# A recurrent layer with an FFN gate on eight cores: the scan's carry is copied by VectorE instead of ScalarE

## The reference

```python
xn = layernorm(x)                                   # over the 1024 features
# linear recurrence with complex states, one per p of 1024
Lambda = exp(-exp(nu_log) + 1j * exp(theta_log))
Bu = einsum('ph,blh->blp', (B_re + 1j*B_im) * exp(gamma_log)[:, None], xn)
xs = scan over l of  s[l] = Lambda * s[l-1] + Bu[l]
s  = einsum('hp,blp->blh', C_re + 1j*C_im, xs).real + D * xn
# gate
g  = silu(relu(xn @ W1 + b1) @ W2 + b2)             # 1024 -> 4096 -> 1024
out = x + s * g
```

## Time and profile before

| | us |
|---|---|
| two timed runs | 4930.87 and 5070.12, median 5000.49 |
| the profiled execution | 4701.79 |
| its span, slowest core (core 4) | 4700.7 |
| spans of the eight cores | 4659.5 to 4700.7 |

### The profile page before, as it was taken

How to read it: one execution, slowest core, us unless ns; L and a number is a source line. 1 busy time by engine, 2 the same in 40 slices (tenths; PEclk the granted TensorE clock), 3 DMA queues, 4 the chain that set the end, 5 groups by cost and what they waited for, 6 DMA issues and landing times.

```text
span 4700.7 us, 61388 instructions; the slowest of 8 cores (4659.5 to 4700.7 us)
## 1 busy us (share of the span) xinstructions
PE 3147.0 (67%) x21664; PEld 2267.8 (48%) x21760; DVE 2185.4 (46%) x3385; ACT 1035.5 (22%) x2150; POOL 22.0 (0%) x46
## 2 busy tenths in 40 slices
PE   2303587594949668584967858495875949496698
PEld 1102274463728355462836446272745637283567
DVE  5740644436373543537354353736344363725301
ACT  3003131221213122131213113121312212121222
POOL 0010000000000000000000000000000000000000
PEclk9755788797979879796988979797987979698789
DMA  4865274463728355471926447282744637283566
GB/s 139 195 142 150 72 233 161 152 207 100 259 72 265 130 181 178 132 237 66 288 101 206 156 158 233 73 286 72 236 159 156 202 107 252 72 271 124 170 202 220
DMA packets 409228, 800.92 MB, mean 170 GB/s; under 512 B 50528, under 2 KB 50528, under 8 KB 406880
## 3 DMA queue, kind: packets, MB, share of 16 engines
q1 hardware_dynamic: 361184, 738.26, 48.2%
q10 hardware_dynamic: 41984, 41.95, 2.6%
q0 software_dynamic: 5760, 16.78, 2.3%
HBM read 755.01 MB, written 58.72 MB: 173 GB/s over the span
## 4 chain that ended last, share of the span: by engine, by line
PE 49%; DVE 32%; ACT 6%; issue 6%; DMA 5%; DVEq 1%; ACTq 1%; SPq 0%; POOLq 0%; POOL 0%
PE PB L764 19%; PE PB L558 10%; PE PA L804 9%; PE PB L804 7%; DVE vv L633 3%; DVE vv L638 3%; DVE s_b L835 3%; DMA h<-W 3%; DVE vv L710 2%; DVE vv L704 2%; DMA sc_w<-h 2%; DVE g_b L709 2%; DVE tmp L697 2%; DVE g_b L699 2%; DVE tmp L707 2%
## 5 line engine op out<-in xcount | busy, mean ns | idle before, releaser
L764 PE MATMUL PB<-xnf,wslot 128*128 128x256 bf16 x8192 | 1022.8, 293 | 830.8 <-ACT h L774 603.0
L764 PEld LDWEIGHTS PB<-xnf,wslot 128*128 128x128 bf16 x8192 | 856.0, 105 | 999.7 <-issue 849.8
L835 DVE SCALAR_TENSOR_TENSOR s_b<-xnf,d_tab,s_b 128x256 f32<-128x256 bf16 x256 | 124.0, 484 | 1394.1 <-ACT g_b L818 1370.2
L774 ACT ACTIVATE h<-PB,b_tab 128x256 bf16<-128x256 f32 x1024 | 485.7, 474 | 560.7 <-PE PB L764 553.0
L804 PE MATMUL PA<-h,wslot 128*128 128x256 bf16 x4096 | 474.0, 275 | 44.6 <-ACT h L774 44.6
L804 PE MATMUL PB<-h,wslot 128*128 128x256 bf16 x4096 | 474.3, 275 | 0.0
L804 PEld LDWEIGHTS PA<-h,wslot 128*128 128x128 bf16 x4096 | 401.3, 98 | 101.5 <-issue 52.7
L804 PEld LDWEIGHTS PB<-h,wslot 128*128 128x128 bf16 x4096 | 403.8, 99 | 49.4
L642 ACT ACTIVATE carry<-vv 128x1 f32<-128x1 f32 x128 | 26.0, 203 | 1550.2 <-DVE vv L638 1550.2
L681 PE MATMUL PA<-xnf,wslot 128*128 128x512 bf16 x992 | 267.7, 428 | 100.4 <-DVE vv L710 98.7
L558 PE MATMUL PB<-xsre,wslot 128*128 128x512 bf16 x976 | 258.8, 406 | 28.4 <-DMA wslot<-sc_c 22.4
(11 more groups left out here) (87 smaller groups left out, 2631.7 us busy)
## 6 DMA issues: line engine op xcount, KB each, us to landing
wslot<-sc_w SPq DMA_DIRECT2D x256, 2048.0 KB, 10.5
wslot<-sc_b SPq DMA_DIRECT2D x32, 2048.0 KB, 10.2
wslot<-sc_c SPq DMA_DIRECT2D x32, 2048.0 KB, 10.9
xsl<-x SPq DMA_DIRECT2D x32, 1024.0 KB, 5.2
out<-xsl ACTq DMA_DIRECT2D x32, 1024.0 KB, 4.8
h<-W POOLq DMA_DIRECT2D x8, 1024.0 KB, 13.0
sc_w<-h SPq DMA_DIRECT2D x8, 1024.0 KB, 8.2
h<-W POOLq DMA_DIRECT2D x32, 256.0 KB, 4.7
```

The lines of the kernel that those rows point to most:

```text
L764: inst = nc.tensor.matmul(bank[:, 0:256], pslot(jw)[:, kk * 1024 + ml * 128: kk * 1024 + (ml + 1) * 128], xnf_p[:, kk * NSUP + sub * NSUB: ...
L774: ev = S(lambda m2=mi, b=bank: nc.scalar.activation(h1[:, m2 * NSUB:(m2 + 1) * NSUB], b[:, 0:256], AF.Relu, bias=b1_tab[:, m2:m2 + 1]))
L835: nc.vector.scalar_tensor_tensor(s_b[:, m2 * NSUP + sub * NSUB: m2 * NSUP + sub * NSUB + NSUB], xnf_p[:, m2 * NSUP + sub * NSUB: m2 * NSUP ...
```

## The change

The two copies of the last column to `carry` are made by DVE (`tensor_copy`) instead of ACT (`activation` with Identity), directly behind the scans. With them go the wait of ACT for the second scan, and four kinds of waits of DVE for ACT's copies: before the first scan of each m, before `vv` is written anew, and before `emit_rot` uses `vv[0]`. Order on DVE alone now protects `carry` and `vv`.

```diff
@@ emit_rot
         rt = vv[0][:, 0:NSUP]
-        VX(SE, carry_s[6])
         for m in range(CH):
@@ emit_rest, in the chain
                 vii = vv[m % 3][:, NSUP:2 * NSUP]
-                VX(SE, carry_s_prev[m])
                 rb, vrb = bass.broadcast_tensor_aps(r_tab[:, m:m + 1], vrr)
...
-                SX(VE, m_sc)
-                S(lambda mm=m, a=vrr: nc.scalar.activation(
-                    carry[:, 2 * mm:2 * mm + 1], a[:, NSUP - 1:NSUP],
-                    AF.Identity))
-                carry_s[m] = S(lambda mm=m, a=vii: nc.scalar.activation(
-                    carry[:, 2 * mm + 1:2 * mm + 2], a[:, NSUP - 1:NSUP],
-                    AF.Identity))
+                V(lambda mm=m, a=vrr: nc.vector.tensor_copy(
+                    carry[:, 2 * mm:2 * mm + 1], a[:, NSUP - 1:NSUP]))
+                V(lambda mm=m, a=vii: nc.vector.tensor_copy(
+                    carry[:, 2 * mm + 1:2 * mm + 2], a[:, NSUP - 1:NSUP]))
@@ the backward part, in the loop over m
-                if m >= 3:
-                    VX(SE, carry_s[m - 3])
-                else:
-                    VX(SE, carry_s_prev[(6, 7, 5)[m]])
                 V(lambda a=vrr: nc.vector.tensor_tensor(
                     a, tmp[0][:, :], tmp[1][:, :], ALU.add))
```

More of the change, by code:

```diff
@@ L273, in build_program @@
     chain_done = 0
-    carry_s = [0] * CH
-    carry_s_prev = [0] * CH
     sevac_last = 0
@@ L636, in emit_rest @@
                 rb2, vib = bass.broadcast_tensor_aps(r_tab[:, m:m + 1], vii)
[L637 to L640, removed]
-                SX(VE, m_sc)
-                S(lambda mm=m, a=vrr: nc.scalar.activation(
-                    carry[:, 2 * mm:2 * mm + 1], a[:, NSUP - 1:NSUP],
-                    AF.Identity))
-                carry_s[m] = S(lambda mm=m, a=vii: nc.scalar.activation(
-                    carry[:, 2 * mm + 1:2 * mm + 2], a[:, NSUP - 1:NSUP],
-                    AF.Identity))
+                V(lambda a=vii, d0=rb2, d1=vib, mm=m:
+                  nc.vector.tensor_tensor_scan(
+                      a, d0, d1, carry[:, 2 * mm + 1:2 * mm + 2],
+                      ALU.mult, ALU.add))
+                V(lambda mm=m, a=vrr: nc.vector.tensor_copy(
+                    carry[:, 2 * mm:2 * mm + 1], a[:, NSUP - 1:NSUP]))
+                V(lambda mm=m, a=vii: nc.vector.tensor_copy(
+                    carry[:, 2 * mm + 1:2 * mm + 2], a[:, NSUP - 1:NSUP]))
                 xr = xsre[:, m * NSUP:(m + 1) * NSUP]
@@ L715, in build_program @@
             emit_rest(CH - 1)
-            carry_s_prev = list(carry_s)
             vmul_mark_prev = vmul_mark
```

## The result

The changed kernel takes 4102.04 us (median of 11 runs, 4078.34 to 4506.44); beside it the kernel before took 4878.3 us (median of 10, 4674.7 to 5070.12). The ratio is 0.8745, 95% interval 0.8703 to 0.8786: 12.5% faster. The profiled executions took 4084.92 us and, before, 4701.79 us.

The account below looks back on a forecast made before the run. Bound: PE waiting for relus stuck in ACT's in-order queue behind the chain's carry copies. 15 x 39.2 = 588 us off 4701.8 gives 4114 (0.875); off 4930.9, about 4340 for the metric; 8-in-10 range 4090 to 4520.

Parts of the forecast that it names:

- the cause: W1's start: PE waits 603.0 us, 15 times, for relus queued on ACT behind carry copies that wait for DVE's scans.
- Rival C: At W1: DVE's chain end, not ACT's queue, releases PE, so the stall stays; 69 us slower, 5069 us; chance 0.04.
- A copy at 0.27 us from start to start: DVE's chain: each 128x1 carry copy costs 0.27 us, taken from 128x2 operations; 4.3 us per step.
- 4 x 0.54 = 2.2 us: DVE's chain: copies of m = 0 to 3 delay the release of W1's third group by 2.2 us per step.
- 3.6 + 25.5: W1 on PE: first 16 matmuls take 3.6 us, the other 224 take 25.5, with 1.3 us of slow-clock start saved.
- the 39.2 us carry through: After W2's start: instructions keep the same predecessors, so the whole gain of 39.2 us per step is kept.
- A step takes 234 us instead of 273.4: Whole step, as a sign of being right: its length falls from 273.4 to 234 us.
- The chain under the Silu: Before W2's Silu: the chain ends 3.3 us before the Silu could start, so stays hidden up to 0.47 us per copy.
- Nothing from step 0: Step 0: no gain, since ACT waits 87.04 us for a C_re load, which also hides 4.3 us of copies.
- the basis for the metric: Whole kernel: 588 us taken off the middle known execution, 4930.9 us, giving 4343, say 4340, rather than 4114.
- Rival A: PE's clock: without the stall's rest the lower clock is held through, costing up to 513 us, 4627 at most; chance 0.14.
- Rival B: A new wait: late W1 weight pieces, 3.5 us per step, 53 us, 4393; or copies above 0.47 us each; chance 0.07.

Follow-up runs that it names:

- Experiment 1: The changed kernel with one wait added: ACT waits for the second scan of m = 7 before W1's first relu; ratio 1.0114 to the kernel before, profiled 4751.02 us.
- experiment 2: The kernel before with only the carry copies of m = 6 and 7 moved to DVE, 12 of 16 still on ACT; profiled 4445.66 us, no ratio.
- experiment 3: The kernel before with the carry copies on GpSimd instead of ACT, DVE waiting for GpSimd instead; ratio 0.8924, profiled 4187.54 us.
- experiment 5: The changed kernel with one DVE copy of two elements instead of two copies per m; ratio 0.8727 to the kernel before.
- experiment 8: The changed kernel run once more, unaltered, on another chip; 4114.1 to 4482.93 us, no ratio.

## Why the prediction was right, point by point

**Right: the cause.** ACT's in-order queue was the stall. Experiment 1 shows it by putting back that wait alone, experiment 2 by its size at a place in between, experiment 3 by keeping everything else. Rival C (the stall stays) had a chance of 0.04 and is out.

**Right: the sum on the profiled basis.** Forecast 4701.8 - 588 = 4114, ratio 0.875; measured 4084.9, ratio of timed runs 0.8745. That these two ratios agree so closely is in part luck: the gain between the two profiles is 617 us and not 588, so they alone give 0.869. By its terms:
- A copy at 0.27 us from start to start: 0.26.
- "4 x 0.54 = 2.2 us" of copies ahead of the release of W1's third group: 1.54. The count was wrong, three m's and not four (experiment 5).
- The 240 matmuls, "3.6 + 25.5" and 1.3 to W2, 30.4 us in all: 29.4. The 240 matmuls took 28.1 us against 3.57 + 26.82 before, so 2.3 us of slow start were saved, more than the 1.3 that I took and than the 1.9 that I called all of it.
- Per step 39.2 forecast; on this pair of profiles 71.8 - 29.4 - 1.5 = 40.9 us. Between the starts of two chains the mean is 269.9 us before and 230.4 after, 39.5 less. It is less than 40.9 because of something that I had put at nothing with "the 39.2 us carry through": on this core (2) five of the changed kernel's fourteen rounds take 231 to 235 us and not about 229, and in these five the start of Bu runs partly at the 1.2 GHz level; Bu needs 6.2 us up to the chain's start where the quick rounds need 3.6. A sixth (233 us) has a wait of Cx for a weight load, 3.2 us. (One quick round, 229.0 us, has 5.3 us at that place, so this does not account for every microsecond.) Windows of PE (length, busy time with count, granted clock, DMA share, GB/s) at the start of Bu, in a slow and in a quick round:

```profile
1193.60:1199.90 6.30, 6.27 (x17) 0.57 0.09 33
1658.00:1662.00 4.00, 3.91 (x19) 1.00 0.45 164
```

  In the kernel before, 13 of the same 14 starts were granted 1.00 on core 4. Why the clock is low there in some rounds stays open.
- The rest of the 617 us lies in the profile of before: from the last chain's start to the end core 4 took 415.9 us, at a granted clock of 0.82 in its first W2 and in most of what follows, where core 6 took 390.6. That is 25 us of the basis 4701.8 that no step of the kernel needs. Core 6, which was free of it there,

```profile
core 6: 4659.5 us, clock 0.831
```

  took 4053.4 us after the change (below): 606 us less, 15 x 40.4, where 588 was forecast.
- "A step takes 234 us instead of 273.4": the window of 273.35 us is longer than the mean round, 269.9; 39.2 off that is 230.7, and 230.4 was measured.
- The chain under the Silu: forecast 3.3 us of room, measured 1.8. W2 came earlier than forecast, and the chain's end did not. The point from which copies show was forecast at 0.47 us per copy; that working left out that dearer copies delay W1, and with it the Silu, too. With this taken in, the forecast's own numbers give 0.27 + 3.3 / 8 = 0.68, and the measured ones 0.26 + 1.8 / 10 = 0.44 (an estimate; ten of sixteen copies lie behind W1's release). That 0.47 comes near is two errors that cancel.
- Nothing from step 0: the second chain starts at 508.4 us, against 506.8 before; these are two different cores, and core 4 has 505.6 and 506.8. As said.
- Rival C's price used 16 steps (69 us) and 256 copies (0.39 us each); only 15 steps have a stall, so 65 us and 240 copies would have been right. Nothing hangs on it.

**Too high: the basis for the metric.** The step that failed is "I put it at the middle one of the three known executions". The number on record, 4340, adds 229 us to the profile's 4114 for a lower clock; the median over 11 runs is 4102. It was a guess about how often the clock is lowered, made from three executions, of which two happened to be hit. In ten runs of the kernel before the three lowest are 4674.7, 4679.1 and 4740.3 us, and the median is 4878.3, 177 us above the profile; in the changed kernel the median is only 17 us above the profile. The stated range held the result at its low end, and by luck: 4102 is 12 us above its lower bound of 4090, and four of the eleven runs are below it.

**Rival A (the lower clock is held through)** did not come: the cores of the changed kernel's profile lie within 30 us of each other, at 0.879 to 0.882 of the clock:

```profile
core 2: 4083.8 us, clock 0.881
core 4: 4078.3 us, clock 0.879
core 6: 4053.4 us, clock 0.882
```

Two of its 11 runs (4423.27 and 4506.44 us) lie 340 and 420 us up, under the 513 that I gave as the most it could cost; the cores of the die that was hit have mean clocks of 0.757 to 0.782 there. The denser PE work did not make such runs the rule. What sets them off stays open; no run here varied it. In the profile of experiment 8, the changed kernel again, core 3 has short stretches near 0.81 in nearly every step. Here are two windows of it, both inside one burst of W1:

```profile
2428.00:2434.00 6.00, 6.00 (x48) 0.81 0.76 240
2434.00:2440.00 6.00, 6.00 (x57) 0.99 0.86 290
```

So the limiter rule of the Trainium skill ("TensorE: Matmul & The Clock Gate", Part 1), which speaks for A, agrees with some stretches of some executions; in the changed kernel's first profile no core has such a stretch of 3 us or more, although all eight run the same dense work.

**Rival B (weights, dear copies)**: PE waited for a weight piece of W1 once, 2.8 us in all, where 3.5 us in every step was the rival's price, and the copies were not dear. Out.

## What to carry to other kernels

Before an operation is put on an engine because it is idle there, look at what is queued behind it: a copy of one column cost 40 us per step on an engine that was busy for 22% of the span, because it waited for a long chain in front of evictions that did not. Moving it to another idle engine moves the question, as GpSimd's start shows, and once that queue was free too GpSimd was the better place by 19 us. The engine that produces the operand needs no wait of another engine, but its own path must have room, and here the room was 1.8 us per step. When a queue is freed, count the instructions ahead of the next release in emission order, not by index.

## What the runs showed of the hardware that I had not expected

A copy of one element per partition, 128x1 in fp32, took 0.154 us on DVE, 0.203 on ACT and mostly 0.65 on GpSimd (0.18 for four of 256 in experiment 3), and the one with two elements 0.17 on DVE. GpSimd's longer copies did not slow DVE: its operations kept 0.69 us, and the way from the chain's start to W1's third group was 51.49 us in experiment 3, as in the kernel before (51.48).
